# GpSimd's constants, crossings and tridiagonal matrix of an eigenvector computation, in other places of its order

## The reference

```python
# layer 0: three graph convolutions, weighting = adj * adj
h = jnp.maximum(_layernorm(x, axis=-1), 0.0)
h = jax.nn.relu(_slconv(h, adj, S, W1))      # 256 -> 512
h = jax.nn.relu(_slconv(h, adj, S, W2))      # 512 -> 1024
x = x + _slconv(h, adj, S, W3)               # 1024 -> 256
# layer 1: in the basis of the eigenvectors U of the normalised Laplacian of adj
_, U = jnp.linalg.eigh(L_norm)
h = jnp.maximum(_layernorm(x, axis=-1), 0.0)
agg = jnp.einsum('mn,bnd->bmd', U.T, h)
out = jax.nn.relu(agg @ W1 + b1) @ W2 + b2
x = x + jnp.einsum('nm,bmd->bnd', U, out)
```

## Time and profile before

| | |
|---|---|
| median of 3 runs (lowest to highest) | 2244.22 us (2244.05 to 2244.74) |
| profiled execution: its time / its span | 2244.8 us / 2243.0 us |
| TensorE, weight loads, VectorE, ScalarE, GpSimd busy | 98%, 88%, 85%, 55%, 60% |
| mean granted TensorE clock | 0.997 of full speed |
| chain that ended last | TensorE 93%, of it L1786 76% and L1991 (layer 1) 10% |

### The profile page before, as it was taken

The page is one execution under the profiler, slowest core; times in us unless marked ns, Lnnn a source line. Parts: engine busy times, 40 slices in busy tenths (PEclk is TensorE's granted clock), DMA queues, the critical chain, the costliest instruction groups (busy, mean ns, idle before and its releaser), DMA issues.

```text
span 2243.0 us, 48683 instructions
## 1 busy us (share of the span) xinstructions
PE 2208.9 (98%) x12904; PEld 1974.2 (88%) x12904; DVE 1907.7 (85%) x10565; ACT 1223.3 (55%) x3081; POOL 1354.4 (60%) x2103
## 2 busy tenths in 40 slices
PE   7999999999999999999999998999999999999999
PEld 5788888888888888888888887999999999899998
DVE  7889999888888888888777788969999999567776
ACT  5556656666565555555555553555555555345554
POOL 6566666666666666666666667664666666343332
PEclk9999999999999999999999999999999999999999
DMA  3000000000000000000000000000000001024443
GB/s 106 29 29 23 17 29 29 30 29 21 28 30 30 29 24 19 26 28 28 28 28 28 28 29 20 30 29 11 30 28 28 28 29 39 21 84 134 133 131 108
DMA packets 90038, 90.24 MB, mean 40 GB/s; under 512 B 5376, under 2 KB 89088, under 8 KB 89856
## 3 DMA queue, kind: packets, MB, share of 16 engines
q1 hardware_dynamic: 89856, 88.23, 12.3%
HBM read 54.66 MB, written 33.55 MB: 39 GB/s over the span
## 4 chain that ended last, share of the span: by engine, by line
PE 93%; DVE 2%; ACT 2%; POOL 1%; issue 1%; DMA 0%; SPq 0%; ACTq 0%; DVEq 0%; POOLq 0%
PE ps L1786 76%; PE ps L1991 10%; PE ps L1691 4%; PE ps L2001 1%; PE ps L1934 1%; ACT squares L914 0%; DVE A L1182 0%; ACT hid L974 0%; ACT root_s L916 0%; PE ps L1795 0%; POOL w3sum L720 0%; ACT res L962 0%; PE ps L1820 0%; DVE xrow_sb L1191 0%; DMA xl<-in_x_dram 0%
## 5 line engine op out<-in xcount | busy, mean ns | idle before, releaser
L676 POOL COPY Eb<-sc 128x1 f32<-128x1 f32 (+1 forms) x254 | 47.4, 187 | 411.2 <-DVE v L1207 211.7
L1786 PE MATMUL ps<-hid2T,xin 128*128 128x256 f32 x1024 | 237.7, 383 | 8.7 <-issue 8.7
L1786 PE MATMUL ps<-agg2T,w 128*128 128x256 f32 x1024 | 240.4, 380 | 1.9 <-ACT agg2T L962 1.8
L1786 PE MATMUL ps<-weightT,hid 128*128 128x256 f32 x1024 | 234.3, 380 | 1.1 <-ACT hid L979 1.1
L1786 PEld LDWEIGHTS ps<-hid2T,xin 128*128 128x128 f32 x1024 | 191.2, 192 | 35.1 <-issue 9.0
L1786 PEld LDWEIGHTS ps<-agg2T,w 128*128 128x128 f32 x1024 | 188.9, 190 | 30.8 <-ACT agg2T L962 5.7
L1786 PEld LDWEIGHTS ps<-weightT,hid 128*128 128x128 f32 x1024 | 189.7, 191 | 26.1 <-ACT hid L979 1.9
L962 ACT ACTIVATE hid2T<-ps 128x512 f32<-128x512 f32 x256 | 150.6, 589 | 87.6 <-PE ps L1786 86.7
L962 ACT ACTIVATE agg2T<-ps 128x512 f32<-128x512 f32 x218 | 128.0, 594 | 116.9 <-PE ps L1786 115.5
L1385 DVE SCALAR_TENSOR_TENSOR ahead<-ps,ne,ahead 128x14 f32<-128x14 f32 (+1 forms) x1020 | 189.8, 228 | 0.0
L1382 DVE RECIPROCAL ps<-ahead 128x14 f32<-128x14 f32 (+1 forms) x1024 | 188.1, 230 | 0.1
(11 more groups left out here) (401 smaller groups left out, 6513.2 us busy)
## 6 DMA issues: line engine op xcount, KB each, us to landing
xl<-in_x_dram SPq DMA_DIRECT2D x64, 256.0 KB, 2.9
xr<-in_x_dram SPq DMA_DIRECT2D x64, 256.0 KB, 2.9
x_dram<-xr SPq DMA_DIRECT2D x64, 256.0 KB, 2.3
xin<-x_dram SPq DMA_DIRECT2D x64, 256.0 KB, 2.8
out_dram<-xin SPq DMA_DIRECT2D x64, 256.0 KB, 2.4
w<-in_L_gnn_W_dram SPq DMA_DIRECT2D x1, 2048.0 KB, 11.0
w<-in_L_gnn_W_dram SPq DMA_DIRECT2D x1, 1024.0 KB, 12.4
w<-in_L_gnn_W_dram SPq DMA_DIRECT2D x1, 512.0 KB, 6.3
```

The costliest lines, as they stand in the source:

```text
L676: pool.tensor_copy(Eb[:, bass.ds(k, 1)], sc[:, 4:5])
L1786: ins = pe.matmul(dst, a, b, start=start, stop=stop, skip_group_check=plan_.units[i][0][0] in "HPG")
```

## The change

The fourteen selects that build `halves` go into the steps of pair 21: the memset behind the reflector's copies of step 0, and one pair of selects behind those of each of the steps 1 to 7, ahead of the pair's sums there. Pairs 22 and 23 are taken out of GpSimd's loop and written out. The five operations for `T` stand in pair 22 behind the second scale, ahead of the adds; the seven products for `crossed` stand at the same place of pair 23. No operation is added or taken away, and no engine but GpSimd has another order.

```diff
+            def half_ones(l):
+                half = 2 ** l
+                first_halves = halves[:, l, :].rearrange("p (m h r) -> p m h r", h=2, r=half)[:, :, 0, :]
+                whole = ones[:, 0:P // 2].rearrange("p (m r) -> p m r", r=half)
+                pool.affine_select(out=first_halves, in_=whole, compare_op=ALU.is_ge, fill=0.0, base=-half,
+                                   pattern=[[-2 * half, P // (2 * half)], [0, half]],
+                                   channel_multiplier=1).then_inc(halved, 1)
+                pool.wait_ge(halved, 2 * l + 2)
+                pool.affine_select(out=first_halves, in_=first_halves, compare_op=ALU.is_ge, fill=0.0,
+                                   base=2 * half - 1, pattern=[[2 * half, P // (2 * half)], [0, half]],
+                                   channel_multiplier=-1).then_inc(halved, 1)
...
+                    if isinstance(t, int) and t == WITH_STEPS - 1 and s == 0:
+                        pool.memset(halves[:, :, :], 0.0).then_inc(halved, 1)
+                        pool.wait_ge(halved, 1)
+                    if isinstance(t, int) and t == WITH_STEPS - 1 and 1 <= s <= TREE:
+                        half_ones(s - 1)
...
-            pool.memset(halves[:, :, :], 0.0).then_inc(halved, 1)
-            pool.wait_ge(halved, 1)
-            for l in range(TREE):
...
-            pool.wait_ge(halved, 2 * TREE + 1)
-            pool.wait_ge(gram_saved, 1)
-            for l in range(TREE):
-                pool.tensor_tensor(crossed[:, l, :, :], gramV[:, :, :],
-                                   halves[:, l, :].unsqueeze(1).to_broadcast([P, 2, P]), ALU.mult).then_inc(crossed_s, 1)
-            pool.wait_ge(tri_v, 1)
...
+            def crossings():
+                pool.wait_ge(halved, 2 * TREE + 1)
+                pool.wait_ge(gram_saved, 1)
...
+            def build_t():
+                pool.wait_ge(tri_v, 1)
...
+                    if behind_norms and (kind, n) == ("scale", 1):
+                        behind_norms()
...
-            with pool.Fori(WITH_STEPS, PAIRS - 1) as t:
+            pair_sums(WITH_STEPS, True, behind_norms=build_t)
+            pair_sums(WITH_STEPS + 1, True, behind_norms=crossings)
+            with pool.Fori(FIRST_ROUND, PAIRS - 1) as t:
                 pair_sums(t, True)
```

More of the change, by code:

```diff
@@ L887, in ln2_scalars, with pair_sums @@
                 pool.tensor_tensor(rs[:, s, 3, :], rs[:, s, 2, :], coef[:, 3, :], ALU.mult).then_inc(ln2_p, 1)
-            def pair_sums(pair, more, plan_=LATE):
+            def crossings():
+                pool.wait_ge(halved, 2 * TREE + 1)
+                pool.wait_ge(gram_saved, 1)
+                for l in range(TREE):
+                    pool.tensor_tensor(crossed[:, l, :, :], gramV[:, :, :],
+                                       halves[:, l, :].unsqueeze(1).to_broadcast([P, 2, P]), ALU.mult).then_inc(crossed_s, 1)
+            def build_t():
+                pool.wait_ge(tri_v, 1)
+                all_of = lambda t, n: t.unsqueeze(1).to_broadcast([P, NB, n])
+                pool.tensor_tensor(T[:, :, :], ident[:, :, :], all_of(Db[:, :], N), ALU.mult).then_inc(t_built, 1)
+                pool.tensor_tensor(Zt[:, :, 0:N - 1], ident[:, :, 0:N - 1], all_of(Eb[:, 0:N - 1], N - 1), ALU.mult).then_inc(t_built, 1)
+                pool.tensor_tensor(Zsq[:, :, 0:N - 1], ident[:, :, 1:N], all_of(Eb[:, 0:N - 1], N - 1), ALU.mult).then_inc(t_built, 1)
+                pool.wait_ge(t_built, 3)
+                pool.tensor_tensor(T[:, :, 1:N], T[:, :, 1:N], Zt[:, :, 0:N - 1], ALU.add).then_inc(t_built, 1)
+                pool.wait_ge(t_built, 4)
+                pool.tensor_tensor(T[:, :, 0:N - 1], T[:, :, 0:N - 1], Zsq[:, :, 0:N - 1], ALU.add).then_inc(t_built, 1)
+            def pair_sums(pair, more, plan_=LATE, behind_norms=None):
                 for kind, n in SUMS_ORDER:
```

## The result

The changed kernel takes 2232.79 us (median of 5 runs, 2232.41 to 2233.52), the kernel before 2244.36 us beside it (5 runs, 2244.05 to 2244.85). The ratio is 0.995, 95% interval 0.9939 to 0.9961: 11.57 us less, where 11.94 were forecast, and within the stated range. The profiled execution spans 2231.0 us instead of 2243.0. Measured inside the traces, from the start of P1 of pair 22 to the end of the span, it is 863.36 us before and 2231.0 - 1379.59 = 851.41 us after: 11.95 us (spans are given to 0.1 us, so such differences hold to about 0.1 us).

The account below looks back on a forecast made before the run. TensorE, busy 98% of the span, bounds the kernel. Its hole in pair 22 (8.81 us) and the slowed clock (3.13 us) give 11.94 us, other terms 0: 2244.22 - 11.94 = 2232.3 us, range 2230.8 to 2236.2 us.

Parts of the forecast that it names:

- The hole and the clock: Pair 22: P5 8.81 us late, waiting for GpSimd's first turn; P5 to P3 3.13 us longer at lower clock; 11.94 us regained.
- What is next late for P5: Pair 22: the first turn still needs `agg2` evacuated; it starts at 1380.52 and ends 1.3 us before P5 is due.
- The slack of VectorE's strand: VectorE's 18.0 us wait at L1425 for spread counts shrinks by 11.9; 6.1 us slack stay, so all 11.94 us count.
- The masks: Steps of pair 21: 6.3 us of memset and selects; VectorE loses 0 to 0.2 us around step 8, path cost 0.
- T and the crossings: Pairs 22 and 23: late adds covered by spares of 1.6, 0.8, 0.5 us (P4, G1, G6); cost 0, at most about 0.5.
- Rival 1: Steps of pair 21: masks hold VectorE's column chain by ports or late copies; 5.7 us lost, 2238.0 us; chance 0.04.
- Rival 2: Pair 22: T's lag reaches TensorE, up to 5.4 us plus 3.1 us of clock, 2240.8 us at worst; chance 0.05.
- rival 3: Pairs 22 and 23: both lags pass through ScalarE's queue and stop two products; 3.6 us slower, 2247.8 us; chance 0.02.
- Rival 4: Pair 22: the hole ahead of P5 isn't GpSimd's, something else ended it; nothing changes, 2244.2 us; chance 0.03.

Follow-up runs that it names:

- crossings alone: Changed kernel with only the seven products for `crossed` moved, into pair 23; masks and T stay ahead of pair 22: 2239.67 us.
- one, three, six more: Changed kernel with one operation for T repeated one, three or six times in pair 22, delaying its adds: 2233.89, 2237.22 and 2241.57 us.
- masks in step 7: Changed kernel with all seven pairs of selects in step 7 of pair 21 instead of one pair in each of steps 1 to 7: 2237.31 us.
- all into idle time: Changed kernel with selects behind the sums of steps 10 to 12 of pair 21, crossings behind pair 22, T behind pair 23, where GpSimd idles: 2233.05 us.
- masks alone: Changed kernel with only memset and selects moved, into the steps of pair 21; crossings and T stay ahead of pair 22: 2238.74 us.
- T alone: Changed kernel with only the five operations for T moved, into pair 22; masks and crossings stay ahead of pair 22: 2235.73 us.

## Why the prediction was right

**The hole and the clock (11.94 us).** The trace gives 11.95 us from P1 to the end. The waits were put down to GpSimd by the code and by 0.10 us between two rows; the three single moves show it, since each shortens the hole by what it takes out of GpSimd's block (T 8.81 to 2.48, the crossings to 3.94; the masks to 4.07, less than their 6.6 us for the reasons found there).

**What is next late for P5.** The turn starts at 1380.46 (1380.52 worked out) and P5 on time.

**The slack of VectorE's strand.** 6.1 us worked out, 6.0 left, and this agreement is luck. The prediction had VectorE's work ahead of the wait unmoved. In truth the counts were saved 1.93 us sooner (1465.83 instead of 1467.76), as GpSimd's memset, selects and crossings no longer lay beside their preparation (the first operation on `Eb` took 0.71 us instead of 1.49). Behind them one short operation, which reads two tensors from SBUF, took 5.02 us instead of 0.28. The rows are that operation before and in the changed kernel, and GpSimd's second node operation there:

```profile
1467.85 0.28 DVE L1413 SCALAR_TENSOR_TENSOR dgs<-gramV,ident 128x128 f32<-128x128 f32 x1
```
```profile
1465.92 5.02 DVE L1425 SCALAR_TENSOR_TENSOR dgs<-gramV,ident 128x128 f32<-128x128 f32 x1
```
```profile
1470.87 0.72 POOL L739 TENSOR_TENSOR h<-h,aggT 128x256 f32<-128x256 f32 x1
```

In the changed kernel GpSimd works from the crossings (1448.07) without a pause until 0.08 us ahead of this second node operation; before, it idled 0.4 to 1.0 us ahead of each add (the first is in the earlier trace rows). The operation of VectorE ends 0.06 to 0.08 us behind the start of that node operation in all six kernels with the crossings in pair 23, whenever it began: it took 5.02, 8.90, 6.11, 8.72, 13.16 and 5.02 us (changed, crossings alone, one, three, six more, masks in step 7), and the wait was 6.0 us in each of them. With six more:

```profile
1465.77 13.16 DVE L1428 SCALAR_TENSOR_TENSOR dgs<-gramV,ident 128x128 f32<-128x128 f32 x1
```

So the 6.0 us are set by where GpSimd's order first pauses, and not by 18.0 less 11.9. With the crossings elsewhere it took 0.57 us (all into idle time), 0.63 us (masks alone) and 1.28 us (T alone), and the wait was 9.6 to 10.2 us. Why it got through so soon there, although GpSimd had no pause just then either, no run shows. The change does hold VectorE up; it costs nothing because there was slack left.

**The masks.** The tight place was step 8's copies: worked out to end at 1352.2 us, they ended at 1352.16; VectorE waited 0.18 us (0 to 0.2), and its idle time covered it. The masks in step 7 show what that cover is worth.

**T and the crossings.** The first add of pair 22 starts 14.86 us after P5 (14.9 worked out), fin 5 begins 1.54 us ahead of G1 and ends 0.9 us ahead of it (0.8), the fourth left ends 0.5 us ahead of G6 (0.5). Kernels with a longer lag put holes at these places and no others.

**Rivals.** Rival 1 fell with L1267's durations and with the equal time from step 6 to P1. The Trainium skill's rule of the exclusive lock of the SBUF ports ("SBUF — State Buffer", section "SBUF: two separate sides") isn't refuted by that: it names VectorE operations with two inputs in SBUF or in a two-port mode, and by the code none in a step reads two tensors from SBUF. Behind the steps this case's traces show such a hold. With the masks alone moved, VectorE prepares the counts beside the crossings and T; in the changed kernel it does so while GpSimd is idle. The rows are an operation of 128x256 and one of 128x1, each with the masks alone moved and then in the changed kernel:

```profile
1378.46 0.83 DVE L1343 TENSOR_TENSOR tmp<-Db,pad 128x256 f32<-128x256 f32 x1
...
1381.10 0.88 DVE L1347 TENSOR_TENSOR ext<-ext 128x1 f32<-128x1 f32 x1
```
```profile
1375.54 0.42 DVE L1341 TENSOR_TENSOR tmp<-Db,pad 128x256 f32<-128x256 f32 x1
...
1377.37 0.16 DVE L1345 TENSOR_TENSOR ext<-ext 128x1 f32<-128x1 f32 x1
```

So a small operation isn't safe by being small. And the holds of 5.02 to 13.16 us above lasted longer than one operation of GpSimd, 1.27 us, so the rule's one whole instruction is not their upper limit. Beside the selects, in the kernel before, the same operation of 128x256 kept 0.43 us, though the selects read SBUF too; there the trace doesn't show the rule. Rival 2 is a real mechanism, as the longer lags show, and needs one operation more to begin; the path of rival 3, through ScalarE's queue to P4, shows from three more on, and only pair 22 was tested for it. Rival 4 fell with the result.

**What was off.** The median moved by 11.57 us and not by 11.94. The interval of the ratio (8.8 to 13.7 us) holds both, and the traces give 11.95, so I take the rest for the scatter of the start. In the expectations three terms were mis-sized: the crossings' wait for the Gram matrix and their longer time beside VectorE (masks alone), the 0.1 us of wait between two dependent operations (one and three more), and the sum of lag and clock (six more). The term of the prediction that was right only in its number is VectorE's slack.

## What to carry to other kernels

Work of an off-path engine that nobody wants soon must not stand ahead of what the bounding engine wants next; put it behind that, and then check every queue that the new place delays, with the spare of each, as here 0.5 to 1.6 us at three places. Look at the durations on the other engines as well as at their waits: work that fills GpSimd's pauses stretched one operation of VectorE from 0.28 to 5.02 us, which no wait shows. Once the hole is short enough the clock's share goes with it, so the last part of such a move can bring more than the first. When a hole's end reads "issue", compare its end with the ends of the operations on the other engines that the code waits for.

## What the runs showed of the hardware

**The clock after a hole.** P5 and P6 take 6.90 us at full clock. After holes of 2.5, 3.9, 4.1 and 8.8 us they took 6.98, 9.68, 9.64 and 10.03 us. The price rises steeply between the first and the second, and hardly after that. The granted clock was 1.00 in the window behind the first (T alone) and 0.72 from 1388.4 to 1398 us behind the hole of 4.1 (masks alone).

**The same hole doesn't always have the same price.** In the first steps TensorE stands 1.97 to 2.02 us for `qcol`, at the same place of each of the ten profiled executions. In the profiled execution of the changed kernel the window behind it is at full clock; in that of "one operation more", which has the 2.02 us, it is at 0.87, and the twelve matmuls from that step row to the next take 1.5 us longer. First the window of the changed kernel, then the other one:

```profile
60.00:70.00 10.00, 10.00 (x63) 8.62 (x62) 9.52 (x48) 5.64 (x15) 9.98 (x10) 1.00 0.18 54
```
```profile
60.00:70.00 10.00, 10.00 (x48) 8.46 (x48) 8.48 (x39) 5.42 (x12) 9.58 (x10) 0.87 0.16 52
```

The very first matmuls of layer 0 scatter as well, 5.14 us and 6.40 us for the same sixteen (4.82 to 6.40 us in the ten executions); the windows over them read a clock of 1.00 in both, so the cause isn't shown:

```profile
12.73 5.14 PE L1832 MATMUL ps<-weightT,h 128*128 128x256 f32 x16
```
```profile
12.68 6.40 PE L1835 MATMUL ps<-weightT,h 128*128 128x256 f32 x16
```

Together they put P1 of pair 22 at 1379.59 us in one execution and at 1382.17 us in the other, though nothing that the change touches lies ahead of step 0 of pair 21. In the ten profiled executions the spread lies here; of the others there is no trace, but it is the likely source of their scatter too. So an effect of 1 us is read from the trace, between two points behind the start, and not from the times.
